# Gathering the kept source rows of two edge networks compactly, and moving them to their columns with predicated copies

## What is computed

```
x = _layernorm(x + _L0_gnn_ref(x, edge_weight, edge_attr_3, edge_index, ...))   # radial messages, summed per dst
x = _layernorm(x + _L1_gnn_ref(x, edge_index))                                  # three hops of graph convolution
x = _layernorm(x + _L2_gnn_ref(x, edge_index, edge_attr_32, ...))               # edge network: MLP, max per dst
x = _layernorm(x + _L3_gnn_ref(x, edge_attr3_2x32, src, dst, ...))              # attention over the edges of a dst
```

```
e_feat = jnp.concatenate([x[rol], x[col], edge_attr], axis=-1)
h = jax.nn.relu(e_feat @ W1 + b1)
v = h @ W2 + b2
x_cand = jax.ops.segment_max(v, col, num_segments=num_nodes)
```

## Time and profile before

| what | value |
|---|---|
| runs | 1871.45, 1880.96, 1887.46 us |
| span of the profiled execution | 2207.9 us, mean granted TensorE clock 0.567 |
| busy share | PE 46%, PE weight load 31%, DVE 58%, ACT 22%, POOL 60% |
| gathers of the two edge networks | 392 indirect DMAs, 430.1 us busy |
| scatter of the result | 196 indirect DMAs, 198.3 us busy |
| first edge network, first to last turn | 1270.2 to 1552.5 us |
| second edge network, first to last turn | 1608.4 to 1924.0 us |
| last scatter issued | 2193.1 us |

### The profile page before, as it was taken

The page is one execution under the profiler, slowest core; times in us unless marked ns, Lnnn a source line. Parts: engine busy times, 40 slices in busy tenths (PEclk is TensorE's granted clock), DMA queues, the critical chain, the costliest instruction groups (busy, mean ns, idle before and its releaser), DMA issues.

```text
span 2207.9 us, 14341 instructions
## 1 busy us (share of the span) xinstructions
PE 1022.8 (46%) x3774; PEld 683.9 (31%) x3774; DVE 1273.1 (58%) x2721; ACT 487.1 (22%) x953; POOL 1319.8 (60%) x1251
## 2 busy tenths in 40 slices
PE   7715747645420036144150068877355777501132
PEld 3302313322110036143150034444255767501121
DVE  9845958889525907862438924544834767604610
ACT  7532111111000215141132112222112233201100
POOL 8876666753774075267530366776366667772775
PEclk9955555555555568576575555555555565655555
DMA  7174211110100213131131400000000010100000
GB/s 296 27 270 160 65 21 28 29 25 19 20 13 8 85 40 128 39 118 45 58 140 53 117 3 12 11 20 12 18 20 22 22 25 22 27 12 7 10 12 9
DMA packets 69611, 114.10 MB, mean 52 GB/s; under 512 B 34221, under 2 KB 54170, under 8 KB 68746
## 3 DMA queue, kind: packets, MB, share of 16 engines
q1 hardware_dynamic: 24450, 80.74, 10.5%
q0 software_dynamic: 39104, 12.88, 4.2%
q10 hardware_dynamic: 5960, 19.43, 2.4%
HBM read 64.18 MB, written 55.21 MB: 54 GB/s over the span
## 4 chain that ended last, share of the span: by engine, by line
DVE 39%; PE 20%; another core or an unknown queue 19%; issue 16%; ACT 4%; POOL 1%; DMA 1%; DVEq 0%; ACTq 0%; PEld 0%; POOLq 0%; PEldq 0%
DVE work L1411 12%; DVE work L1422 5%; PE bank L1166 4%; PE bank L1192 4%; DVE A_dst L1411 3%; PE bank L1323 3%; PE bank L1316 3%; DVE stat L1422 2%; PE bank L1241 2%; PE bank L1348 2%; DVE A_sum L1510 1%; PE bank L1279 1%; PE bank L1371 1%; DVE A_tmp L1411 1%
## 5 line engine op out<-in xcount | busy, mean ns | idle before, releaser
L691 POOL DMA_INDIRECT A_src<-table,pos_i x392 | 430.1, 1097 | 336.4 <-DMA table<-A_dst 149.5
L1241 PE MATMUL bank<-w2fold,work 65*128 65x384 f32 x392 | 272.1, 868 | 222.1 <-DVE work L1411 175.5
L1422 DVE TENSOR_REDUCE work<-work 128x80 f32<-128x1280 f32 (+3 forms) x147 | 204.8, 1422 | 139.9 <-ACT work L962 68.0
L691 POOL DMA_INDIRECT A_dst<-in_x,dst_i x196 | 198.0, 1010 | 105.3 <-issue 58.8
L832 POOL DMA_INDIRECT out<-A_dst,out_i x196 | 198.3, 1012 | 96.3 <-issue 62.1
L1411 DVE TENSOR_TENSOR work<-bank,work 128x384 f32<-128x384 f32 (+1 forms) x294 | 155.2, 591 | 143.2 <-remote 97.3
L1241 PEld LDWEIGHTS bank<-w2fold,work 65*128 65x128 f32 x392 | 121.2, 329 | 371.3 <-issue 346.8
L1279 PE MATMUL bank<-nodes_w,small 128*128 128x128 f32 (+1 forms) x784 | 130.8, 330 | 140.4 <-issue 69.2
L691 POOL DMA_INDIRECT A_src<-x_pos,A_tmp x140 | 145.3, 1038 | 72.6 <-issue 42.0
L1279 PEld LDWEIGHTS bank<-nodes_w,small 128*128 128x128 f32 (+1 forms) x784 | 119.3, 238 | 151.0 <-issue 76.4
L928 ACT ACTIVATE work<-A_tmp,b1col,w1col 65x256 f32<-65x256 f32 x98 | 58.5, 600 | 445.2 <-PE bank L1241 188.0
(11 more groups left out here) (357 smaller groups left out, 2210.5 us busy)
## 6 DMA issues: line engine op xcount, KB each, us to landing
work<-in_x SPq DMA_DIRECT2D x26, 960.0 KB
x_pos<-A_sum SPq DMA_DIRECT2D x13, 990.0 KB
out<-work ACTq DMA_DIRECT2D x13, 960.0 KB
A_tmp<-ew_turned_rows ACTq DMA_DIRECT2D x49, 130.0 KB
table<-A_dst SPq DMA_DIRECT2D x2, 3136.0 KB
edge_sums<-A_dst SPq DMA_DIRECT2D x2, 3136.0 KB
A_src<-table,pos_i POOLq DMA_INDIRECT x392
table<-A_dst SPq DMA_DIRECT2D x13, 448.0 KB
```

What stands on the lines that cost most here:

```text
L691: pool.indirect_dma_start(out=column(t), out_offset=None, in_=of, in_offset=bass.IndirectOffsetOnAxis(ap=idx[:, t:t + 1], axis=0), bounds_ ...
L1241: last = nc.tensor.matmul(banks[2 * (u % PAIRS_DEEP) + j][:, 0:PATHS], hidT[:, u % PAIRS_DEEP, j * P:(j + 1) * P], w2fold[:], start=True, ...
L1422: return v.tensor_reduce(out=o, in_=a, axis=AX, op=op)
```

## The change

In a window of 28 columns (one chunk) of one partition only the kept edges need a row from the table. The change numbers them: the first 16 columns of a window in the scratch area hold its kept rows, one behind the other, and POOL gathers only these 16 columns (`SLOTS_IN_WINDOW`). That makes 112 gathers for each edge network, where there were 196. The rows land in `compact[layer]`, which is a part of `work` in the first and `A_msg` in the second edge network. DVE moves them to their columns in five steps of 16, 8, 4, 2 and 1 columns (`MOVES`), each a predicated copy under a mask of one byte per edge, and a last one for the rows that don't move. The last two steps write into `A_src`. The masks are made once, in `make_windows`. If any window had over 16 kept rows, the count `n_short` is set to T and the other columns are gathered too.

In the first edge network the moves of window 6 stand before the first turn, those of window 0 behind turn 1, and those of windows 1 to 5 one by one behind turns 7c - 4 to 7c + 1. In the second the moves of window 0 stand before the first turn, and those of window c behind turns 7c - 6 to 7c - 1. POOL's waits for `e_vused` and `a_used` are gone. `spread` before the second edge network uses a part of `work` as scratch. The second short list has one path less.

```diff
+SLOTS_IN_WINDOW = 16
+MOVES = [(16, 12), (8, 20), (4, 24), (2, 26), (1, 27)]
...
-            for k in (3, 4):
+            for slot in range(SLOTS):
+                pool.wait_ge(n_stored[slot], 16 * (D_CHUNKS // 2 + 1))
+            for k, of, order in zip((3, 4), compact, WINDOW_ORDER):
 
                 pool.wait_ge(table_stored, 16 * parts_until(k))
                 pool.wait_ge(gather_ok, k + 2)
 
-                for q in range(QUADS):
-                    here = quad_rows[k - 3][q % SLOTS]
-                    if q >= SLOTS:
-                        pool.wait_ge(here, 64 * (q // SLOTS))
-                    if q >= QUADS_AHEAD:
-                        done_quads = q - QUADS_AHEAD + 1
-                        if k == 3:
-                            pool.wait_ge(e_vused, 4 * done_quads + 4 * SLOTS)
-                        else:
-                            pool.wait_ge(a_used, done_quads + SLOTS)
-                    first = 4 * (quad_of(q) if k == 3 else q)
-                    gather(lambda t: A_src[:, t, :], tables[k], pos_i, edge_limit, lambda t: here,
-                           range(first, first + 4))
...
+                pool.sem_inc(wide_in, 1)
+                for i, c in enumerate(order):
+                    here = window_rows[k - 3][i % SLOTS]
+                    if i >= SLOTS:
+                        pool.wait_ge(here, 16 * SLOTS_IN_WINDOW * (i // SLOTS))
+                    gather(lambda t: of[:, t, :], tables[k], pos_i, edge_limit, lambda t: here,
+                           range(c * GATHER_CHUNK, c * GATHER_CHUNK + SLOTS_IN_WINDOW))
...
+            def make_windows():
...
+                for shift, n in reversed(MOVES):
+                    step(v.tensor_copy(win_bits, win_row))
+                    step(ts(win_bits, win_bits, shift, ALU.bitwise_and))
+                    step(stt(win_moved, win_bits, 0.0, win_row, ALU.is_gt, ALU.mult))
+                    step(tt(win_row, win_row, win_moved, ALU.subtract))
...
             def add_layer0(c):
+                if c == CHUNKS - 2:
+                    make_windows()
                 v.wait_ge(dst_rows[c], 16 * GATHER_CHUNK)
...
+            def move_window(layer, c, k):
+
+
+                rows, base = compact[layer], c * GATHER_CHUNK
+                if k == 0:
+                    i = WINDOW_ORDER[layer].index(c)
+                    v.wait_ge(wide_in, layer + 1)
+                    v.wait_ge(window_rows[layer][i % SLOTS], 16 * SLOTS_IN_WINDOW * (i // SLOTS + 1))
+                if k == len(MOVES):
+                    all_of = slice(base, base + GATHER_CHUNK)
+                    step(v.copy_predicated(A_src[:, all_of, :], bcast(move_masks[0][:, c, :], FEAT), rows[:, all_of, :]))
+                    return
+                shift, n = MOVES[k]
+                to = A_src if shift == 1 else rows
+                step(v.copy_predicated(to[:, base + shift:base + shift + n, :][:, ::-1, :],
+                                       bcast(move_masks[shift][:, c, ::-1], FEAT), rows[:, base:base + n, :][:, ::-1, :]))
...
+                for c in range(1, CHUNKS - 1):
+                    for k in range(len(MOVES) + 1):
+                        after.setdefault(7 * c - 4 + k, []).insert(0, partial(move_window, 0, c, k))
+                after.setdefault(1, []).append(partial(bring_window, 0, 0))
+                bring_window(0, CHUNKS - 1)
                 pipeline(v, bring_rows, None, None, take, after=after)
...
-            spread(A_sum, A_dst, A_msg, count["carry"])
+            spread(A_sum, A_dst, spare_rows, count["carry"])
...
+                bring_window(1, 0)
                 after, late = in_time([
+                    *((f"move_{k}", lambda c, k=k: move_window(1, c, k), range(1, CHUNKS)) for k in range(len(MOVES) + 1)),
                     ("soft_max", soft_max, early), ("weights", weights, early),
```

More of the change, by code:

```diff
@@ L437, in gnn_kernel @@
         assert maxima_until(EARLY - 1) < T
-        HOOKS = dict(soft_max=12, exp_scores=13, weights=13, exp_rows=14, normalise=15, turn=16, take_turned=17, product=18,
+        HOOKS = dict({f"move_{k}": k - len(MOVES) - 1 for k in range(len(MOVES) + 1)}, soft_max=12, exp_scores=13, weights=13, exp_rows=14, normalise=15, turn=16, take_turned=17, product=18,
                      take_product=19, sums=20, add=21, square=22, variance=23, root=24, scale=25)
@@ L1699, in make_short @@
                 step(ts(kept, spare[:, 0:T], SKIP / 2, ALU.is_lt))
+                step(v.memset(in_window, 1.0))
+                step(v.memset(by_window(in_window)[:, :, 0:1], 0.0))
+                step(scan1(run, kept, in_window))
+                step(total(carry[:, 0:1], run, ALU.max))
+                step(ts(carry[:, 0:1], carry[:, 0:1], float(SLOTS_IN_WINDOW), ALU.is_gt, float(T), ALU.mult))
                 v.memset(kept[:, 0:1], 1.0)
@@ L1728, in make_short @@
                 step(ts(short_row_i, spare[:, 0:T], float(SKIP), ALU.add))
-                done(total(spare[:, 0:1], kept), count_ready, 1)
+                step(total(spare[:, 0:1], kept))
+                done(tt(spare[:, 0:1], spare[:, 0:1], carry[:, 0:1], ALU.max), count_ready, 1)
                 v.wait_ge(count_turned, 1)
@@ L2054, in _ @@
             seq_after = count["seq"] + 10
-            with v.If(n2 > FEW2):
+            with v.If(n2 > FEWEST2):
                 use_short_list()
@@ L2351, in _ @@
                 v.sem_inc(msg_ready, EARLY)
+                for c in range(CHUNKS):
+                    bring_window(1, c)
                 pipeline(v, bring_both, None, score)
```

82 lines of the change are left out of this document (60 added, 22 removed).

## The result

The changed kernel takes 1852.68 us (1845.55 to 1860.04, four runs) where the kernel before takes 1881.43 (1871.45 to 1887.46): a ratio of 0.9851, 95% interval 0.9816 to 0.9886. That is 28.8 us less, where 4 were forecast, and inside the stated range. Ratios leave out the executions of a kernel that were over 1.5% slower than its fastest, so a ratio isn't always the quotient of the two medians given.

The account below looks back on a forecast made before the run. POOL was taken to bound the first network's gathers and the scatter; after the change, DVE's turns, then the scatter's tail. Masks and lists 1.6 + 6, first network +26, end -38 give -4 on 1880.96: 1877 us, range 1840 to 1925.

Parts of the forecast that it names:

- The two sorts of time, and the 327 us: The span was 327 us over the runs' median; gaps with PE and DVE nearly idle were read as only in the profiled execution.
- The 182 us that were put ahead of 1243: Rest of the 327 us, placed before 1243 on the trace's time axis, where the change moves almost nothing.
- a POOL without pauses starves the others: Rival: gaps are in the runs too, and removing the throttle's pauses slows PE and DVE; 1940 us, chance 0.10.
- faster, 1845: Rival: turns run at the quick ends of their bounds, so POOL's 109 us before the scatter come through; -36 us, chance 0.30.
- Start of the first network: Turns 0, 2 and 4 wait for whole windows, then 44 steps of 4.8 us; last turn at 1534 against 1508, +26 us.
- Start and turns of the second: Turn 2 waits for the 32nd gather at 1632; turns of 83 and 154 us plus 7 of copies, last turn at 1876.
- undisturbed it is between: Second network's 28 turns with chunk steps: 5.5 us each, between 5.07 of DVE busy time and 6.06 beside a busy POOL.
- The end: Scatter ends 180 us after the second network's last turn, 34 of them until chunk 4: 2056 against 2094, -38 us.
- The port, and POOL's step: POOL steps taken as 1.30 and 1.287 us; copies holding off gathers at a shared port would make 1888, but 1877 was kept.
- Masks and lists: Extra operations in make_short, +1.6 us, and in make_windows, 11 to 13 us partly hidden, +6 us.
- The copies' price: Six predicated copies on DVE cost 5.6 us a window; hidden in the first network but for first windows, 7 us in the second.
- the rival of twice the price: Rival: a mask read beside two rows makes copies cost 2.1 ns an element; +56 us, 1933 us, chance 0.09.

## Why the prediction was right, and where it was not

**The two sorts of time, and the 327 us: wrong.** "I read these gaps as time that only the profiled execution has." They are in the traces of three chips, and the times of the runs there are as long as these traces. On the fourth the kernel before is short, and the traces of the two versions run there have no standstills. Taking them out was what made the forecast fit the recorded result, because that came from a chip without them: this was luck, not insight. The trace that I read looks like those of the three. The 182 us that were put ahead of 1243 are more like 215: the changed kernel's first gather comes at 1028.58. The argument from equal sizes (44 and 101 worked out, 182 left over by definition) could not tell "this execution" from "this chip". The rival *a POOL without pauses starves the others* was given 0.10 and 1940 us (its own sum, +68 - 4, makes 1945). For the recorded comparison it is false; on the chip of that kind that ran the changed kernel it is what happens: slower by 2.0%, by the mechanism named (109 us less of POOL against pauses lost), and decided by the experiment that puts the pauses back.

**The outcome between the forecast and its first rival.** 28.8 us less is more than the 19 us that the prediction called no change, so what came is its "faster", given 0.35, and not the 0.40 of "within". 1852.68 lies 24 us from the forecast of 1877 and 8 from the rival *faster, 1845*. But that rival's mechanism didn't come: it wanted turns at the quick ends of the bounds, and they took 5.0 and 6.25 us, at or over the slow ends. The steps below show the parts.

**Start of the first network: right.** The third window was forecast 74 us after the first gather (1318 - 1243.6). DVE goes on at 1105.77, 77 us after 1028.58. The last turn was forecast 290 us after the first gather; it is 297.5. The 44 steps take 220 us, 5.0 each, not 4.8.

**Start and turns of the second: the term with the largest error.** The second window was forecast 53 us after the first gather, and is 47. The 18 turns behind it take 85 us, forecast 83. The 28 with chunk steps take 175, where 154 + 7 were forecast: 6.25 each with the copies in. That is the slow end of the bound, 6.06 beside a busy POOL, and some of the 0.84 us of copies a turn on top (28 x 6.06 + 7 = 177). DVE is busy 154 of the 175 us, 88%, where it was 84% in the earlier trace rows. So "undisturbed it is between" was wrong: the pace of the earlier trace rows is about that of a chip without standstills.

**The end: the right size by another way.** Forecast: last turn + 180. Measured: 1851 - 1662.5 = 189. But chunk 4 isn't waited for. POOL waits for DVE before the first chunk of the scatter, 57.86 us, and 3 us more in two waits at 1616 and 1659; after that it waits for DVE no more. The end is the first chunk's readiness + 279 us of scatter.

**The port, and POOL's step: weighed on the wrong side.** The forecast took 1.30 and 1.287 us a step throughout. Beside DVE's work the steps are 1.40 to 1.43. The earlier trace rows had it: a mean of 1097 ns for the 392 gathers, and so 1.40 with the 0.30 between them, where 0.99 was taken. The lengthening comes from single long DMAs beside DVE, such as this one of the scatter, with the DVE product beside which it starts:

```profile
1628.41 2.02 DVE L1429 TENSOR_TENSOR work<-work,r 128x1792 f32<-128x1792 f32 x1
...
1628.58 2.71 POOL L850 DMA_INDIRECT out<-A_dst,out_i  x1 [0.30 <-issue]
```

The DMA ends 0.86 us behind the product. From 1047 on 44 of POOL's DMAs in this trace take over 1.3 us, and 38 of them end 0.8 to 0.9 us behind a DVE instruction with two SBUF inputs: 19 tensor operations like this one and 19 predicated copies. The Trainium skill (SBUF — State Buffer, Who interferes with whom) has the shared port pair as an exclusive lock, for which such a DVE instruction contends with a GpSimd one that reads SBUF; these rows agree. The longest gather fits less well. It starts at 1036.80, takes 10.31 us, and ends 0.9 us behind a run of 32 DVE scans:

```profile
1031.39 14.84 DVE L1528 TENSOR_TENSOR_SCAN A_sum<-not_last,A_msg 128x196 f32<-128x196 f32 x32
```

Three gathers before it took 1.05 to 1.17 us beside the same scans, and it was held over more than twenty of them, not over one instruction. Why isn't shown.

I used the rule against the change, for its copies. It speaks for it too: 0.12 us on each of the 392 gathers of before is 47 us (an estimate from the two step times; with the mean of the earlier trace rows it is 42) of a path on which POOL was alone, and the changed kernel has POOL's gathers off that path. From the first gather to the end of the scatter the changed kernel takes 822.6 us (1028.58 to 1851.2). The forecast was 794 for it (290 + 27 between the networks + 297 + 180) and 806 for before (264 + 27 + 515). The one is short by 29, measured; the other by about 47, by the estimate. Then the difference grows from 12 to some 30 us, and 28.8 were measured. This agreement is weaker than it looks. No trace of the kernel before on a chip without standstills was taken, so its side is argued, not shown, and its scatter is left at the quiet step: at the 1.43 of the changed kernel's scatter it would add 27 us more, and the sum would come to twice the measured gain. What is shown is the size of the effect from the other side: 48 gathers more in one network cost 9 to 11 us.

**Masks and lists.** With `make_short` POOL waits 45.05 us instead of 43.78 on one chip with traces of both, +1.3. On another it is 42.43 and 44.10 in two versions of the changed kernel instead of 40.78, +1.7 and +3.3. Forecast was 1.6. `make_windows` was forecast at 6 of its 11 to 13 us. On the chip of the recorded comparison it takes 16 us, from 588.7 to 604.8, and costs nothing on DVE's own path, since DVE waits for gathered rows behind it all the same, for chunk 5 and then for the last chunk:

```profile
609.37 1.09 DVE L1429 TENSOR_TENSOR A_dst<-A_dst,A_sum 128x896 f32<-128x896 f32 x1 [4.55 <-DMA A_dst<-in_x,dst_i]
...
647.56 1.09 DVE L1429 TENSOR_TENSOR A_dst<-A_dst,A_sum 128x896 f32<-128x896 f32 x1 [30.98 <-DMA A_dst<-in_x,dst_i]
```

So its cover was whole, as far as its operations don't hold up POOL's gathers in turn, which no run tells. The copies' price was right, and the rival of twice the price is out.

## What to carry to other kernels

When the span of a profile is far from the times of the runs, find out which of them the difference belongs to before taking anything out: run the same kernel again and look at every run's span. A throttle that looks idle (a producer that waits though it could run ahead) may be what keeps the other engines moving on some chips, so when a change makes it unnecessary, try the change with the throttle as well; here that turned 1.020 into 0.952 on one chip, and the turns on the other kind of chip were no longer for it. And when an engine is taken off the path, count its steps at the length they have beside the others (the mean of the whole group in the profile), not at the length in a quiet stretch.

## What the runs showed of the hardware

On three chips, while POOL issues indirect DMAs one every 1.29 to 1.30 us, there are stretches of 70 us and more in which the other engines come almost to a stand: PE at 7 to 11% busy, turns of 56 us instead of about 5. PE then starts matmuls that wait for nothing one every 2.80 us, and ACT's steps are 11.2 and 22.4 us, four and eight times that. The DMA engines are 4 to 5% busy in these stretches, so the transfers don't fill them. In the networks of the changed kernel the standstill begins 60 to 83 us behind the first gather and ends within some 12 us of POOL's last. The changed kernel's scatter, a row as long and nearly as dense (1.44 us a step), has none, so a row of DMAs alone isn't enough. On two chips, pauses of 2 to 12 us between groups of four or more gathers were enough to avoid the long standstills in the networks; single turns of 11 and 18 us near the starts are left. In the recorded comparison's trace, with the same program and nearly the same pace of POOL, PE stays at 88%. The granted clock is 0.50 in the bad and in the good stretch.

What differs between the chips isn't shown, nor is what makes an engine take 2.80 us for an instruction there. The version with pauses wasn't run on a chip of the second kind without its surplus gathers; with them it is 0.989 and 0.991 there.
